# One VectorE instruction that copies attention scores out of PSUM and takes their minimum, and a new split of the half-precision conversions

## The reference

```python
xn = layernorm(x) * ln_w + ln_b            # positions x 192
S = (xn @ Wq.T) @ (xn @ Wk.T).T            # 4096 x 4096 scores, unscaled
attn1 = softmax(S, axis=-1)
attn2 = square(relu(S))
attn = e1/(e1+e2) * attn1 + e2/(e1+e2) * attn2     # e1, e2 = exp(w1), exp(w2)
out = attn @ (xn @ Wv.T) + x
```

## Time and profile before

| | us |
|---|---|
| median of 3 runs (lowest, highest) | 3696.91 (3694.4, 3699.23) |
| the profiled execution, its own time | 3695.92 |
| span of the profiled execution | 3694.1 |
| ScalarE, VectorE, TensorE, GpSimd busy in the span | 2136.1, 2223.8, 3217.1, 1023.0 |

### The profile page before, as it was taken

How to read it: one execution, slowest core, us unless ns; L and a number is a source line. 1 busy time by engine, 2 the same in 40 slices (tenths; PEclk the granted TensorE clock), 3 DMA queues, 4 the chain that set the end, 5 groups by cost and what they waited for, 6 DMA issues and landing times. The chain is left out here.

```text
span 3694.1 us, 47959 instructions
## 1 busy us (share of the span) xinstructions
PE 3217.1 (87%) x16424; PEld 1267.7 (34%) x16424; DVE 2223.8 (60%) x2585; ACT 2136.1 (58%) x2306; POOL 1023.0 (28%) x510
## 2 busy tenths in 40 slices
PE   1249999999999999999999768999998767999997
PEld 0012222222322223222222224555554334555454
DVE  4755254552545524465211356999999547999998
ACT  0016655556555565555666225888888026888786
POOL 0211002111021110210200032555555323555555
PEclk9669999999999999999999879999999889999999
DMA  6220213202131121210200334666666535666666
GB/s 180 47 72 19 58 42 70 50 23 58 40 69 39 37 58 40 65 46 14 58 9 9 81 81 97 128 126 125 129 129 126 128 95 94 129 128 127 128 125 123
DMA packets 691174, 295.71 MB, mean 80 GB/s; under 512 B 603314, under 2 KB 645042, under 8 KB 689266
## 3 DMA queue, kind: packets, MB, share of 16 engines
q1 hardware_dynamic: 690996, 293.45, 37.1%
HBM read 95.46 MB, written 34.28 MB: 35 GB/s over the span
## 5 line engine op out<-in xcount | busy, mean ns | idle before, releaser
L440 ACT ACTIVATE prob<-ps_s,cur 128x1024 f32<-128x1024 f32 x1024 | 1085.4, 1111 | 740.2 <-PE ps_s L514 738.7
L527 PE MATMUL ps_a<-prob,vt 128*64 128x512 f32 x4096 | 996.5, 607 | 0.0
L1335 PE MATMUL ps_s<-kst,qs 128*128 128x512 f16 x2560 | 640.3, 382 | 135.2 <-ACT gp L1184 121.0
L1126 POOL TENSOR_TENSOR p_lo<-gp,p_hi 128x1024 f16<-128x1024 f32 x256 | 547.2, 2138 | 303.1 <-ACT p_hi L1198 292.8
L1348 PE MATMUL ps_o<-v_hl,at_hi 128*128 128x384 f16 x2048 | 548.9, 329 | 10.1 <-DMA at_lo<-p_lo 10.0
L508 PE MATMUL ps_s<-q_a,k_a 128*128 128x512 f16 x2048 | 536.5, 384 | 8.4 <-issue 3.8
L1348 PE MATMUL ps_o<-v_hl,at_lo 128*128 128x192 f16 x2048 | 505.9, 248 | 0.0
L527 PEld LDWEIGHTS ps_a<-prob,vt 128*64 128x64 f32 x4096 | 249.4, 136 | 412.3 <-issue 410.9
L1335 PEld LDWEIGHTS ps_s<-kst,qs 128*128 128x128 f16 x2560 | 231.5, 98 | 402.8 <-ACT gp L1184 163.0
L1573 DVE TENSOR_REDUCE nmx<-ps_s 128x1 f32<-128x1024 f32 x256 | 310.4, 1212 | 28.5 <-PE ps_s L1335 28.5
L508 PEld LDWEIGHTS ps_s<-q_a,k_a 128*128 128x128 f16 x2048 | 138.3, 98 | 519.1 <-ACT prob L440 436.7
(11 more groups left out here) (176 smaller groups left out, 2865.7 us busy)
## 6 DMA issues: line engine op xcount, KB each, us to landing
z<-z_scratch SPq DMA_DIRECT2D x96, 384.0 KB, 3.8
sq<-rn_scratch SPq DMA_DIRECT2D x16, 768.0 KB, 10.3
qs<-q_scratch SPq DMA_DIRECT2D x64, 128.0 KB, 2.5
gn_x<-in_x SPq DMA_DIRECT2D x4, 1536.0 KB, 18.5
z_scratch<-gn_x SPq DMA_DIRECT2D x4, 1536.0 KB, 11.6
q_a<-hi SPq DMA_DIRECT2D x64, 96.0 KB, 2.3
rden<-den_scratch SPq DMA_DIRECT2D x64, 96.0 KB, 2.2
o_scratch<-o_s SPq DMA_DIRECT2D x64, 96.0 KB, 1.9
```

What stands on the lines that cost most here:

```text
L440: act.activation(prob[:, a % PR, :], ps_s[:, a % 2, :], ACT.Exp, bias=cur[:, slot:slot + 1], scale=1.0 / SPLIT).then_inc(exped, 1)
L527: ins = pe.matmul(ps_a[h * HALF:(h + 1) * HALF, j % 2, :], vt[:, slot, m, :], prob[:, a % PR, h * CH:(h + 1) * CH], start=(m == 0), stop=( ...
L1126: pool.tensor_tensor(p_lo[:, cols], prob[s][:, cols], p_hi[:, cols], ALU.subtract).then_inc(lo_made, 1)
L1335: ins = pe.matmul(ps_s[:, c % 2, h * CH:(h + 1) * CH], qs[:, s, qt, :], kst[:, ktile, cols], start=(t == 0), stop=(t == len(terms) - 1))
```

## The change

- A new tile `neg` in SBUF, one row of four chunks. `maximum` becomes one instruction: TENSOR_SCALAR reads the PSUM buffer, multiplies by a negative constant (the sign of `mix[:, 6:7]` and of `top[:, 3:4]` is turned), writes the product to `neg`, and accumulates the minimum over the chunk straight into `nbias`. The two instructions on lines 1573 and 1575 go.
- ScalarE's ReLU and exponential read `neg` in place of PSUM. The exponential's scale is now the constant -1.0 and no longer a value per partition. Each waits for the one instruction.
- TensorE no longer waits for the exponential to have the PSUM buffer back, but for a new semaphore `s_taken`, which VectorE raises after the new instruction with a semaphore instruction of its own. VectorE waits, before it writes a chunk of `neg`, for the exponential of that chunk in the row before.
- `HIGH_ACT` is (2, 3) in place of (1, 3): GpSimd converts chunks 0 and 1, ScalarE chunks 2 and 3. In ScalarE's slot the conversion of chunk 1, ahead of square 2, goes, and that of chunk 2 comes in behind square 3, ahead of ReLU 3.

```diff
-        MX, CO = 2 * NQ + 3, 6
+        MX, CO = NQ + 3, 6
-        HIGH_ACT = (1, 3)
+        HIGH_ACT = (2, 3)
-        nmx = sb("nmx", [P, NQ])
+        neg = sb("neg", [P, NQ, QB])
+        s_taken = sem("s_taken")
...
                     def relu(row, s, c, first=False):
-                        act.wait_ge(mx_op, MX * (RB * b + row) + 2 * c + 1)
+                        act.wait_ge(mx_op, MX * (RB * b + row) + c + 1)
-                        act.activation(sqr[s][:, cols], ps_s[:, c % 2, :], ACT.Relu, scale=top[:, 3:4]).then_inc(relued, 1)
+                        act.activation(sqr[s][:, cols], neg[:, c, :], ACT.Relu, scale=top[:, 3:4]).then_inc(relued, 1)
...
                     def exp_piece(row, s, c, first=False):
-                        act.wait_ge(mx_op, MX * (RB * b + row) + 2 * c + 2)
+                        act.wait_ge(mx_op, MX * (RB * b + row) + c + 1)
-                        act.activation(prob[s][:, c * QB:(c + 1) * QB], ps_s[:, c % 2, :], ACT.Exp,
-                                       bias=nbias[:, s, c:c + 1], scale=mix[:, 6:7],
+                        act.activation(prob[s][:, c * QB:(c + 1) * QB], neg[:, c, :], ACT.Exp,
+                                       bias=nbias[:, s, c:c + 1], scale=-1.0,
...
-                        high(t, s, 1, older and t == 0)
                         square(t, s, 2)
                         if new:
                             relu(t + 1, 1 - s, 2, first)
                             exp_piece(t + 1, 1 - s, 2, first)
                         square(t, s, 3)
+                        high(t, s, 2, older and t == 0)
                         if new:
                             relu(t + 1, 1 - s, 3, first)
...
                     if b:
-                        pe.wait_ge(exped, NQ * RB * b)
+                        pe.wait_ge(s_taken, NQ * RB * b)
...
-                                pe.wait_ge(exped, NQ * (RB * b + row) + c - 1)
+                                pe.wait_ge(s_taken, NQ * (RB * b + row) + c - 1)
...
-                    reach_step(dve.tensor_scalar(top[:, 3:4], top[:, 1:2], GAIN / SPAN, None, ALU.mult))
-                    dve.scalar_tensor_tensor(out=mix[:, 6:7], in0=mix[:, 6:7], scalar=1.0 / SPAN, in1=top[:, 1:2],
+                    reach_step(dve.tensor_scalar(top[:, 3:4], mix[:, 7:8], -GAIN, None, ALU.mult))
+                    dve.scalar_tensor_tensor(out=mix[:, 6:7], in0=mix[:, 6:7], scalar=-1.0 / SPAN, in1=top[:, 1:2],
...
-                    def maximum(row, s, c):
+                    def maximum(row, s, c, first=False):
...
-                        dve.tensor_reduce(nmx[:, c:c + 1], ps_s[:, c % 2, :], AX_X, ALU.max, negate=True).then_inc(mx_op, 1)
-                        dve.wait_ge(mx_op, at + 2 * c + 1)
-                        dve.tensor_scalar(nbias[:, s, c:c + 1], nmx[:, c:c + 1], mix[:, 6:7], None, ALU.mult).then_inc(mx_op, 1)
+                        if not first:
+                            dve.wait_ge(exped, NQ * (RB * b + row - 1) + c + 1)
+                        dve.tensor_scalar(neg[:, c, :], ps_s[:, c % 2, :], mix[:, 6:7], None, ALU.mult, ALU.min,
+                                          accum_out=nbias[:, s, c:c + 1]).then_inc(mx_op, 1)
+                        dve.wait_ge(mx_op, at + c + 1)
+                        dve.sem_inc(s_taken, 1)
```

More of the change, by code:

```diff
@@ L1567, in _ @@
                     low_qv(NCH - 1)
-                    def maximum(row, s, c):
+                    def maximum(row, s, c, first=False):
                         at = MX * (RB * b + row)
                         dve.wait_ge(s_full, b * USE + PRO + NQ * row + c + 1)
-                        dve.tensor_reduce(nmx[:, c:c + 1], ps_s[:, c % 2, :], AX_X, ALU.max, negate=True).then_inc(mx_op, 1)
-                        dve.wait_ge(mx_op, at + 2 * c + 1)
-                        dve.tensor_scalar(nbias[:, s, c:c + 1], nmx[:, c:c + 1], mix[:, 6:7], None, ALU.mult).then_inc(mx_op, 1)
+                        if not first:
[4 more added lines that the diff above has]
+                        dve.sem_inc(s_taken, 1)
                         if c == NQ - 1:
-                            dve.wait_ge(mx_op, at + 2 * NQ)
                             dve.tensor_reduce(nbmin[:, s:s + 1], nbias[:, s, :], AX_X, ALU.min).then_inc(mx_op, 1)
-                            dve.wait_ge(mx_op, at + 2 * NQ + 1)
+                            dve.wait_ge(mx_op, at + NQ + 1)
                             dve.tensor_scalar(m1[:, s:s + 1], nbmin[:, s:s + 1], mix[:, 7:8], -1.0, ALU.mult, ALU.min).then_inc(mx_op, 1)
-                            dve.wait_ge(mx_op, at + 2 * NQ + 2)
+                            dve.wait_ge(mx_op, at + NQ + 2)
                             dve.reciprocal(inv[:, s:s + 1], m1[:, s:s + 1]).then_inc(mx_op, 1)
@@ L1649, in _ @@
                     for c in range(NQ):
-                        maximum(0, 0, c)
+                        maximum(0, 0, c, b == 0)
                     slot(0, 0, 0, True, False, False)
```

## The result

| | before | after |
|---|---|---|
| median of 10 runs each, side by side, us | 3694.80 | 3709.23 |
| ratio after to before (95% interval) | | 1.0034 (1.0024 to 1.0044) |
| span of the profiled execution, us | 3694.1 | 3707.3 |
| time from the first maximum to the last row's, image 0 and image 1, us | 583.66, 583.62 | 589.46, 588.98 |

One of the ten runs of the changed kernel took 4869.97 us at a granted clock of 0.65, against 0.95 in the others, and is left out of the ratio. The kernel became slower by 0.34%, 13 us by the spans. The forecast was 31 us slower. So the direction held, the size did not.

A forecast was written before the change was run, and what follows sets the result against it. VectorE's combines, held by GpSimd's subtractions, set a chain of 19.11 us a slot. 60 slots x 0.61 = + 36.6, less 5 at the starts, took 3695.92 to 3727.5, so 3728 us; own range 3713 to 3743, wide range 3668 to 3740.

The forecast's parts named there:

- c1: The end of combine 1 on VectorE, from which the prediction counted the times in a slot.
- The 0.19: Between combine 3's end and ScalarE's conversion of chunk 3: 0.19 us, taken as a handover and kept unchanged.
- the 5.65: In the kernel before, from the end of combine 1 to the start of GpSimd's subtraction of chunk 2: 5.65 us.
- The step of 0.61: ScalarE's late conversion of chunk 2: its subtraction starts 6.26 us after combine 1 instead of 5.65, each slot 0.61 longer.
- ScalarE's part: From ReLU 2 through exponential, sum read, square and conversion until GpSimd's subtraction of chunk 2: 4.35 us.
- the 1.36 taken: New VectorE instruction until its result is there: 1.28 us plus 0.08 for the accumulator read, about 1.36.
- the gain at the starts: First rows of both images, PSUM released earlier to TensorE: 2.5 us returned per image, 5 in all.
- The 1.28 taken from the slope of the earlier trace: New VectorE instruction on 1024 values: slope of TENSOR_SCALAR from PSUM gave 1.31, the reduction's rate 1.27; 1.28 us taken.
- VectorE first: Combine 3 starts before GpSimd's subtraction of chunk 2 where VectorE's loop doesn't turn, slots 18.22: 3674 us, chance 0.18.
- The mixture: Some slots have combine 3 before GpSimd's subtraction of chunk 2, others after: times from 3674 to 3728 us, chance 0.10.
- The new instruction held: VectorE's new instruction and GpSimd hold each other up: + 1.8 us a slot, at least 3800 us, chance 0.04.
- TensorE as the bound: TensorE sets the slot: needs a slot under 17.3 us, which no order considered gives; no chance of its own.

The follow-up runs named there:

- Ahead of square 3: The changed kernel with ScalarE's conversion of chunk 2 one place earlier, before square 3: 3721.70 us, ratio 1.0071.
- copy only: The changed kernel with the old split (chunks 1 and 3 converted by ScalarE), keeping the new VectorE instruction and TensorE's early release: 3687.93 us, ratio 0.9979.
- the exponential's release: The changed kernel, but TensorE again waits for the exponential before it refills a PSUM buffer: 3713.44 us, ratio 1.0049.
- split only: The kernel before with chunk 2 converted by ScalarE behind square 3, scores still read out of PSUM twice: 3716.02 us, ratio 1.0059.
- the scale and release edits together: The changed kernel with a per-partition scale for the exponential and chunk 3's semaphore instruction moved behind the reciprocal: 3681.23 us, ratio 0.9954.
- the conversion behind ReLU 3: The changed kernel with ScalarE's conversion of chunk 2 one place later, behind ReLU 3: 3620.19 us, ratio 0.9795.
- the scale experiment: The changed kernel with the exponential's scale -1 taken from a tile with a value per partition: 3717.11 us, ratio 1.0052.

## Why the prediction had the direction and not the size

The chain of a slot, term by term, for the two slots above (from c1 at 2510.06 to 2529.46, and on):

| from c1 | predicted | measured, two slots |
|---|---|---|
| to the subtraction of chunk 2 | 6.26 | 6.17, 6.09 |
| it, and combine 3's end behind it | 2.13 + 1.08 | as predicted |
| to the conversion of chunk 3 | 0.19 | 0.04, 0.12 |
| to its subtraction, and that | 1.13 + 2.13 | as predicted |
| to combine 0's end | 2.40 | 2.32, 2.32 |
| combine 1 | 4.40 | 4.40 |
| sum | 19.72 | 19.40, 19.40 |

**The step that failed** is "Everything behind this in the chain is unchanged (combine 3, the conversion of chunk 3, which starts 0.19 after it, `part`, combine 0, combine 1)". The 0.19 was not a handover but ScalarE's queue, which in the kernel before was later than combine 3. A later combine 3 first uses up this slack and only then delays the conversion. 0.04 and 0.12 are left of it: 0.15 and 0.07 of the delay were absorbed. In the second slot the 0.12 is a handover, as the queue was free 0.10 earlier (1.14 behind square 0, not 1.04). In the first the conversion starts 1.06 behind square 0, so that queue and combine came to it within 0.02 of each other. Ahead of square 3 shows the slack most plainly, with a combine that ends 1.05 early and gains nothing.

It also means that "No maximum, and no wait of TensorE, is in this sum except inside the 5.65" was wrong for the kernel before. There the subtraction of chunk 2 and combine 3 did not set the conversion of chunk 3. It hung by ScalarE's queue on ReLU 3 at c1 + 5.63, which waits for maximum 3, and that one stood behind combine 2, held by the subtraction of chunk 1 (the kernel before; ScalarE, GpSimd, VectorE):

```profile
2509.56 1.06 ACT L1198 ACTIVATE p_hi<-gp 128x1024 f16<-128x1024 f32 x1 [0.96 <-DVE gp L1605]
2510.69 2.13 POOL L1126 TENSOR_TENSOR p_lo<-gp,p_hi 128x1024 f16<-128x1024 f32 x1 [2.33 <-ACT p_hi L1198]
2511.68 2.22 DVE L1605 SCALAR_TENSOR_TENSOR gp<-gp,coef,vb 128x1024 f32<-128x1024 f32 x1 [0.35 <-ACT vb L1178]
```

The prediction's sum came out at 19.11 because both ways lead to the same conversion, 0.19 apart, and the 0.19 was put in as a term.

**The step of 0.61 was mis-sized.** It measured 0.52 and 0.44. ScalarE's part was right (4.34 against 4.35). The new instruction's result was there earlier than the 1.36 taken, because the accumulator read overlaps the main instruction (1.20 + 0.08 = 1.28), and the handover was 0.11 or 0.03: ReLU 2 starts 1.39 and 1.31 after maximum 2, not 1.47.

**0.08 came from nowhere in the prediction.** Between `coef`'s end and combine 0 VectorE is idle for 0.04 in every kernel with the copy edit, in place of 0.12 to 0.15, and combine 0 ends 2.32 after the subtraction in place of 2.40, in copy only and with the exponential's release too, and not in split only. Why that idle time is shorter wasn't tried by itself.

Together 0.48 - 0.11 - 0.08 = 0.29 a slot on average, against 0.61, so that the slots cost 17.4 us and not 36.6. That is the miss; the number of slots (60 taken, 58 seen) and the gain at the starts (5 taken, 6.4 measured) were near.

**What held.** The new instruction is not held by GpSimd: 1274 ns on average over all of them, and 1.28 us for the longest of the 182 (of 256) that GpSimd worked beside for over 0.1 us. The row of the page's costliest groups:

```profile
L1576 DVE TENSOR_SCALAR_CACHE_REDUCE neg<-ps_s,mix 128x1024 f32<-128x1024 f32 x256 | 326.1, 1274 | 22.9 <-PE ps_s L1336 22.6
```

The 1.28 taken from the slope of the earlier trace rows was right. The Trainium skill (SBUF — State Buffer, section "Who interferes with whom") leaves the TENSOR_SCALAR that writes out its accumulator off its list of instructions that take the shared pair, and now the trace agrees. GpSimd was first in every row but the last of each image. The conversion of chunk 1 by GpSimd cost nothing, and neither did the early release in the steady state. TensorE's wait for the exponential is gone, and its largest from 2450 to 2650 is now for the output scaling (us in total, times, longest):

```profile
PE ps_t L1359 <- DVE ob L1616: 17.3, 10, 2.1
```

**The rivals.** VectorE first: not here, but the scale and release edits together made it so, at nearly the slot lengths it was given. The mixture: not seen in the changed kernel (every slot has the same order), seen with both edits, where the two orders take turns. The new instruction held: refuted. TensorE as the bound, "no order above gives one": true of the orders that were costed, but the order with the conversion behind ReLU 3 nearly gets there, and it was not among them.

## What to carry to other kernels

When instructions of two engines hold each other up, ask of each pair which one starts first, and write down by how much; if that lead is a tenth of a microsecond, an edit elsewhere decides it, and the slot lengths jump. Where the helper engine has slack, try its instruction behind the one on the path, not just off the path's engine: here one line moved by one place was worth 89 us, and a second one moved the same way lost 30 of them. And before a gap between two instructions is carried on as a handover, check whether the later one starts exactly when its own queue gets to it; if so, the gap is slack, and it absorbs a delay first.

## What the runs showed of the hardware

- A TENSOR_SCALAR of 128 x 1024 out of PSUM with an accumulated minimum takes 1.27 to 1.28 us, as the trace names it TENSOR_SCALAR_CACHE_REDUCE, and its accumulator read takes 0.08, 0.07 to 0.08 of it under the main one. Neither is stretched by GpSimd's work: the longest of the 182 that had GpSimd at work beside them took 1.28.
- When a VectorE combine and a GpSimd subtraction had recorded starts within 0.01 us, the combine waited (3.21). With VectorE 0.08 ahead, the subtraction did (3.20).
- A GpSimd cast waits as well: 2.11 in place of 1.04 behind a combine that started 0.07 earlier (2544.79 and 2544.86).
- A granted clock of 0.91 in one slot and 0.98 over 300 us changed no slot length here, where TensorE was not the bound: the kernel with 1.00 over the same 300 us has the same slots to 0.01.
- Out of SBUF, the exponential with a scale per partition took 1.229 on average from 2300 to 2800 in the scale experiment, and 1.134 with a constant in the changed kernel. The Trainium skill (ScalarE: Activation LUTs, section "What ACT_TABLE_LOAD costs") gives some 93 ns for each such operand, and the trace agrees with 95.
